# A sandwich layer in fp32 halves: one joined score product, k's high half written by ScalarE, and the joining of the weighted halves placed later

## The chip, the cores and the metric

One core of one Trainium2 chip runs the whole program. The metric is device time in microseconds of one execution; the number given is the median of the runs. TensorE (PE) multiplies and transposes, VectorE (DVE), ScalarE (ACT) and GpSimd (POOL) do the elementwise work, and SyncE (SP) issues the DMAs.

## The reference

x is 4 batches of 512 tokens, 1024 wide, 16 heads of 64. The program computes, all in fp32:

```
h = layernorm(x)
q, k, v = h @ Wq, h @ Wk, h @ Wv;  rotary embedding on q and k
attn = softmax(causal(q k^T) / 8);  a = (attn @ v) @ Wo
x = x + layernorm(a)
scores = 8 * softmax(layernorm(x) @ Wr^T + br)          # 8 experts
f = sum over experts of scores * ((h2 @ A^T) @ B), rank 16, times 2
out = x + layernorm(f)
```

## The kernel before, in words

An fp32 product is made of products of halves: each operand is split into a high half (a rounded copy) and a low half (the operand less the high half), and a product takes three terms: high with high, low with high, high with low. ScalarE makes the high half by a copy, VectorE or GpSimd the low one by a subtraction.

The attention part runs in 34 slots. A slot u belongs to one pair of heads (128 columns) and one batch; b = u mod 2 names the batch within the half of x that lies in SBUF. Slots 0 to 15 work on the first two batches, 16 to 31 on the other two. Each slot has 8 steps. In a step TensorE does 9 products of the projection of slot u (k, q and v of the pair of heads, 72 in all, three groups of 24), with the attention of the slot before woven in: the scores of one query tile of 128 rows (tile q = 0 to 7: head 0's four query tiles, then head 1's), the transposes of the probabilities of two tiles earlier, and twice a slot the product with v. A score tile i of a head has 128 * (i + 1) columns of keys, because of the causal mask. Step s of slot u works on score tile s - 1 of the slot before (`trailing(u, s, 1)`), so head 0's first tile comes in step 1 and head 1's in step 5.

Scores: `q_hl` holds q's high half in 64 partitions and its low half in the other 64. `k_hh` holds k's high half twice, in both halves of the partitions, so that one product gives (q high + q low) with k high. `k_lo` holds k's low half in its own partitions; the other 64 hold zeros, so that the second product adds q high with k low. Both go to the same columns of one bank and add up there.

The order of the work of each engine is written out by hand, step by step, in a function `slot` of each engine; every engine takes its instructions strictly in that order, and semaphores tie them. Per step and score tile the rank is:

- VectorE `negate` (line 1053): adds the mask to the scores, scales, writes them to `prob`, and gives the negated maximum of each row;
- ScalarE `exponent` (740): exponential with the row sum;
- VectorE `invert` (1063): reciprocal of the sum; GpSimd `divide` (595): the probabilities;
- TensorE `turn_probs` (1499) two steps later; ScalarE `pt_high` (751) and VectorE `pt_low` (1071) split the transposed tile.

Around it, in ScalarE's order: `v_raw` in step 0, `o_lower` (784) in steps 1 and 5, `v_high` in 2, `q_high` (761) in 3, `k_high` (766, both heads) in 6, and the high halves of the next weights (733) in steps 0, 4 and 6 (4 and 6 only with b = 1). In VectorE's: `rotate` (1080, the rotary embedding) in steps 3 and 6, `q_low` (1085) in 4 and 5, `k_low` (1091, 1092) of head 0 in 7 and of head 1 in step 0 of the next slot, `o_add` (1105) in 1 and 6. `o_lower` copies the lower product of the probabilities with v out of the bank, `o_add` adds it to the upper one. GpSimd makes the weights' sums (606, 607) and low halves (613), in steps 1 (b = 0), 2, 4, 5 and 7 (b = 1).

Slots 2 to 9 (`ahead`) also normalise and transpose the x of the other two batches: `x_variance`, `x_scale`, `ln_start`, `x_normal` and `hold_chunk` (in steps 4 and 7). In these slots `k_low` of head 0 stands before `invert` in step 7, in the others after `pt_low`.

Of the kernel before, what the change touches and what calls it, by code (L numbers as in the profile page):

```python
# [18 lines left out]
F32 = mybir.dt.float32  # L19
F32R = mybir.dt.float32r  # L20
# [4 lines left out]
P = 128  # L25
# [42 lines left out]
def sandwich_kernel(nc, x, wqkv, wo, ar, bt, br, cos, sin, scratch, out):  # L68
    with ExitStack() as ctx:
        def sb(stack, name, shape, dt=F32):  # L70
            return stack.enter_context(nc.sbuf_tensor(name, shape, dt))

        def sem(name):
            return ctx.enter_context(nc.semaphore(name))
# [61 lines left out]


        q_hl = sb(sB, "q_hl", [P, 2, 2, SEQ], F32R)
        k_hh = sb(sB, "k_hh", [P, 2, 2, SEQ], F32R)
        k_lo = sb(sB, "k_lo", [P, 2, 2, SEQ], F32R)  # L140
        w_sum = sb(sB, "w_sum", [P, EMBED])
        rope = sb(sB, "rope", [P, SEQ])
        rot = sb(sB, "rot", [P, SEQ])
# [9 lines left out]
        rinv = sb(sB, "rinv", [P, 4])  # L153
        o_low = sb(sB, "o_low", [DH, SEQ])
        o_sum = sb(sB, "o_sum", [DH, 2, SEQ])

        hold_hi = xin[:, 1, :].rearrange("p (c t) -> p c t", c=KC)
        hold_lo = xn[:, 1, :].rearrange("p (c t) -> p c t", c=KC)
# [63 lines left out]
        qk_lo_done = sem("qk_lo_done")  # L222
        s_done = sem("s_done")
        neg_done = sem("neg_done")
        exp_done = sem("exp_done")
        inv_done = sem("inv_done")
        prob_done = sem("prob_done")
# [66 lines left out]
        def real(u):  # L294

            return not isinstance(u, int) or 0 <= u < UNITS
# [399 lines left out]
        def _(act):  # L696
# [64 lines left out]
                    act.activation(q_hl[own, b, h, :], rot[own, :], ACT.Copy).then_inc(qk_hi_done, 1)  # L761

            def k_high(u, b, h):
                own = slice(DH * h, DH * h + DH)
                act.wait_ge(rot_done, 2 * u + 2)
                act.activation(k_hh[own, b, h, :], rot[own, :], ACT.Copy).then_inc(qk_hi_done, 1)

            def v_raw(u, b):
# [31 lines left out]
            def slot(pair, b, half, ahead=False):  # L800
# [6 lines left out]
                for s in range(STEPS):  # L807
                    exponent(u, s)
                    if s == 0 and real(u - 1):
                        v_raw(u - 1, 1 - b)  # L810
                    if s == 1 and real(u - 2):
                        o_lower(u - 2, 0)
                    if s == 5 and real(u - 2) and not (isinstance(u, int) and u > UNITS):
                        o_lower(u - 2, 1)
                    if s == 2 and real(u - 1):
                        v_high(u - 1, 1 - b, fill)
                    if prepares(u, ahead) and s == 6:
                        ln_start(ahead_tile(u) + 1)
                    pt_high(u, s)
                    if real(u):  # L820
                        if s == 0 and b == 0 and late(n, 1):
                            w_high(2, n)
                        if s == 3:
                            q_high(u, b)
                        if s == 6:
                            k_high(u, b, 0)
                            k_high(u, b, 1)
                        if b == 1 and not (isinstance(u, int) and u == UNITS - 1):
                            if s == 6:
                                w_high(1, n + 1)  # L830
# [157 lines left out]
        def _(dve):  # L988
# [56 lines left out]
            def negate(u, s):  # L1045
                a, q, g = trailing(u, s, 1)
                if real(a):
                    n = P * (q % QT + 1)
                    dve.wait_ge(s_done, g + 1)
                    if late(g, 4):  # L1050
                        dve.wait_ge(t_done, g - 3)
                    dve.sem_inc(gate_dve, 1)
                    dve.tensor_tensor_reduce(prob[:, q % 4, 0:n], sc_ps[q % 2][:, 0:n], mask[:, SEQ - n:SEQ],  # L1053
                                             -SOFT, 3e38, ALU.add, ALU.min, nmax[:, q % 4:q % 4 + 1]
                                             ).then_inc(neg_done, 1)

# [29 lines left out]
                                  ALU.subtract).then_inc(qk_lo_done, 1)  # L1086

            def k_low(u, b, h):
                own, other = slice(DH * h, DH * h + DH), slice(DH * (1 - h), DH * (1 - h) + DH)
                dve.wait_ge(qk_hi_done, 4 * u + 3 + h)  # L1090
                dve.tensor_tensor(k_lo[own, b, h, :], rot[own, :], k_hh[own, b, h, :].bitcast(F32), ALU.subtract)
                dve.tensor_copy(k_hh[other, b, h, :], k_hh[own, b, h, :]).then_inc(qk_lo_done, 1)  # L1092

            def v_low(u, b):
                dve.wait_ge(v_hi_done, u + 1)
# [28 lines left out]
            def slot(pair, b, half, ahead=False):  # L1124
# [4 lines left out]
                for s in range(STEPS):  # L1129
# [4 lines left out]
                        if s in (3, 6):  # L1134
                            rotate(u, b, s // 6)
                    closing = isinstance(u, int) and u >= UNITS
                    if s == 1 and real(u - 2) and not closing:
                        o_add(u - 2, 0)
                    if s == 6 and real(u - 2) and not (closing and u > UNITS):
                        o_add(u - 2, 1)  # L1140
                    leads = ahead or (isinstance(u, int) and u == UNITS - 1)
                    if leads and s == 7:
                        k_low(u, b, 0)
# [5 lines left out]
                    pt_low(u, s)  # L1149
                    if s == 0 and not closing and real(u - 1):  # L1150
                        k_low(u - 1, 1 - b, 1)
                    if closing and s == 1 and real(u - 2):
                        o_add(u - 2, 0)
                    if real(u):
                        if s in (4, 5):
                            q_low(u, b, s - 4)
                        if s == 7 and not leads:
                            k_low(u, b, 0)
# [240 lines left out]
        def _(pe):  # L1399
# [76 lines left out]
            def scores(u, s, b):  # L1476
                a, q, g = trailing(u, s, 1)
                if real(a):
# [5 lines left out]
                    if late(g, 2):  # L1484
                        pe.wait_ge(neg_done, g - 1)
                    qc, kc = slice(P * i, P * i + P), slice(0, P * i + P)
                    products(sc_ps[q % 2][:, kc], [(q_hl[:, ab, h, qc], k_hh[:, ab, h, kc]),
                                                   (q_hl[:, ab, h, qc], k_lo[:, ab, h, kc])], True, True
                             ).then_inc(s_done, 1)

            def turn_probs(u, s):
                a, q, g = trailing(u, s, 3)
# [270 lines left out]
```

## Time and profile before

| | us |
|---|---|
| median of 3 runs (1069.21 to 1069.33) | 1069.33 |
| the profiled execution's own time | 1069.58 |
| its span, first to last instruction | 1067.8 |
| TensorE busy | 1049.9 (98%) |
| VectorE busy | 756.9 (71%) |
| ScalarE busy | 591.3 (55%) |
| GpSimd busy | 439.4 (41%) |

The granted TensorE clock was 0.998 of full speed over the span. The attention slots run from about 41 us to 830 us. The ends of products are modelled in the profile, so the distance from start to start says what a product costs, and the busy share of TensorE is not its share of peak.

### The profile page before, as it was taken

The page shows a single profiled execution, that of the slowest core. Times are in us where ns is not written, and L with a number is a line of the kernel's source. Part 1 is how long each engine was busy: PE and PEld are TensorE (multiplying, and loading weights), DVE is VectorE, ACT ScalarE, POOL GpSimd, SP SyncE. Part 2 cuts the span into 40 slices and gives each one's busy share as a digit, 9 for nine tenths or more (in the row PEclk, how much of TensorE's full clock was granted, in tenths as well). Part 3 has the DMA queues.
Part 4 walks back from the last instruction along what each step waited for, and adds up shares of the span by engine and source line. Part 5 has one row for each costly group of instructions (what it writes and reads, how often), then busy time and mean ns, then how long its engine had stood idle before and what let it go on. Part 6 is the DMA issues. An engine that isn't in the chain of part 4 may idle for free.

```text
span 1067.8 us, 20069 instructions
## 1 busy us (share of the span) xinstructions
PE 1049.9 (98%) x5559; PEld 871.3 (82%) x5559; DVE 756.9 (71%) x2138; ACT 591.3 (55%) x1390; POOL 439.4 (41%) x422
## 2 busy tenths in 40 slices
PE   7999999999999999999999999999999999999996
PEld 6888888888888888888888888888877888888884
DVE  8777777776666666666666666666766877777777
ACT  7556666666555665565555655555576333333334
POOL 4153443435353635444452625344457232333221
PEclk9999999999999999999999999999999999999999
DMA  7022324241311256021111112020333323322311
GB/s 280 36 84 70 128 69 128 74 129 55 104 51 34 95 182 227 10 71 33 52 49 31 52 29 69 10 69 17 87 132 93 108 88 107 118 99 87 109 61 60
DMA packets 58663, 90.36 MB, mean 85 GB/s; under 512 B 3568, under 2 KB 36336, under 8 KB 58608
## 3 DMA queue, kind: packets, MB, share of 16 engines
q1 hardware_dynamic: 58464, 89.44, 25.9%
q8 instruction: 25, 0.41, 0.2%
q14 instruction: 30, 0.25, 0.1%
q10 hardware_dynamic: 144, 0.26, 0.1%
HBM read 64.52 MB, written 25.17 MB: 84 GB/s over the span
## 4 chain that ended last, share of the span: by engine, by line
PE 90%; DVE 3%; issue 2%; ACT 2%; POOL 0%; DVEq 0%; ACTq 0%; POOLq 0%
PE bank L1472 46%; PE bank L1403 25%; PE bank L1499 6%; PE bank L1518 3%; PE bank L1517 3%; PE bank L1633 2%; PE bank L1610 1%; PE bank L1445 1%; PE bank L1634 1%; PE bank L1520 1%; PE bank L1433 1%; ACT prob L740 1%; DVE prob L1053 0%; DVE k_hh L1092 0%; PE bank L1415 0%
## 5 line engine op out<-in xcount | busy, mean ns | idle before, releaser
L595 POOL TENSOR_SCALAR prob<-prob,rinv 128x128 f32<-128x128 f32 (+3 forms) x256 | 150.5, 588 | 436.8 <-DVE rinv L1063 436.8
L1472 PE MATMUL bank<-big_hi,w_hi 128*128 128x512 f32 (+1 forms) x776 | 329.4, 424 | 0.3 <-DVE big_lo L1034 0.3
L740 ACT ACTIVATE prob<-prob,nmax 128x128 f32<-128x128 f32 (+3 forms) x256 | 144.0, 562 | 304.3 <-DVE nmax L1053 302.7
L1472 PE MATMUL bank<-big_hi,w_lo 128*128 128x512 f32 (+1 forms) x776 | 304.5, 392 | 0.0
L1472 PE MATMUL bank<-big_lo,w_hi 128*128 128x512 f32 (+1 forms) x776 | 302.1, 389 | 0.0
L1472 PEld LDWEIGHTS bank<-big_hi,w_lo 128*128 128x128 f32 x776 | 145.6, 188 | 33.2
L1071 DVE TENSOR_TENSOR pT_lo<-bank,pT_hi 128x128 fp32r<-128x128 f32 (+3 forms) x256 | 123.7, 483 | 56.0 <-ACT pT_hi L751 53.3
L1472 PEld LDWEIGHTS bank<-big_hi,w_hi 128*128 128x128 f32 x776 | 146.6, 189 | 16.5 <-issue 0.4
L1472 PEld LDWEIGHTS bank<-big_lo,w_hi 128*128 128x128 f32 x776 | 147.1, 190 | 11.6
L1063 DVE RECIPROCAL rinv<-rsum 128x1 f32<-128x1 f32 x256 | 40.8, 159 | 129.3 <-ACT prob L740 128.9
L1053 DVE CUSTOM_DVE_ANT_0 prob<-bank,mask 128x128 f32<-128x128 f32 (+3 forms) x256 | 124.1, 485 | 9.2 <-PE bank L1403 5.1
L1499 PE MATMUL bank<-ident,prob 128*128 128x128 f32 x640 | 112.0, 273 | 1.5 <-POOL prob L595 1.0
L751 ACT ACTIVATE pT_hi<-bank 128x128 fp32r<-128x128 f32 (+3 forms) x256 | 108.8, 425 | 2.1 <-PE bank L1499 0.5
L1499 PEld LDWEIGHTS bank<-ident,prob 128*128 128x128 f32 x640 | 82.9, 141 | 32.5 <-POOL prob L595 6.0
L674 POOL TENSOR_TENSOR res<-res,x 128x1024 f32<-128x1024 f32 x14 | 33.4, 2389 | 146.1 <-ACT res L705 146.1
L613 POOL TENSOR_TENSOR w_lo<-w_sum,w_hi 128x1024 fp32r<-128x1024 f32 x32 | 83.0, 2593 | 8.0 <-ACT w_hi L733 7.7
L1403 PE MATMUL bank<-k_lo,q_hl 128*128 128x128 f32 (+3 forms) x256 | 82.2, 321 | 0.0
L1403 PE MATMUL bank<-k_hh,q_hl 128*128 128x128 f32 (+3 forms) x256 | 80.7, 315 | 0.5 <-DVE k_hh L1092 0.5
L1403 PE MATMUL bank<-big_hi,w_hi 128*128 128x512 f32 x192 | 79.5, 414 | 0.0
L1403 PE MATMUL bank<-big_lo,w_hi 128*128 128x512 f32 x192 | 75.2, 391 | 0.0
L1403 PE MATMUL bank<-big_hi,w_lo 128*128 128x512 f32 x192 | 75.0, 391 | 0.0
L1105 DVE TENSOR_TENSOR o_sum<-bank,o_low 64x512 f32<-64x512 f32 x64 | 43.3, 677 | 37.5 <-ACT o_low L784 37.5
(146 smaller groups left out, 1927.7 us busy)
## 6 DMA issues: line engine op xcount, KB each, us to landing
w_raw<-in_wqkv SPq DMA_DIRECT2D x48, 512.0 KB, 4.4
attention_out<-o_sum SPq DMA_DIRECT2D x64, 128.0 KB, 2.3
w_raw<-attention_out SPq DMA_DIRECT2D x16, 512.0 KB, 4.8
land<-in_x SPq DMA_DIRECT2D x16, 512.0 KB, 3.7
out<-res SPq DMA_DIRECT2D x14, 512.0 KB, 2.6
xin<-in_x SPq DMA_DIRECT2D x12, 512.0 KB, 5.7
xT_hold_hi<-xin SPq DMA_DIRECT2D x8, 512.0 KB, 3.6
xT_hold_lo<-xn SPq DMA_DIRECT2D x8, 512.0 KB, 5.4
```

The source lines that it names most:

```text
L595: pool.tensor_scalar(p, p, rinv[:, q % 4:q % 4 + 1], 1.0, ALU.mult, ALU.mult).then_inc(prob_done, 1)
L613: pool.tensor_tensor(w_lo[:, m, :], src, w_hi[:, m, :].bitcast(F32), ALU.subtract).then_inc(w_lo_done[m], 1)
L674: pool.tensor_tensor(res[:, i, :], res[:, i, :], x1[:, i, :], ALU.add).then_inc(res_done, 1)
L740: act.activation(prob[:, q % 4, 0:n], prob[:, q % 4, 0:n], ACT.Exp, scale=-1.0, bias=nmax[:, q % 4:q % 4 + 1], accum_out=rsum[:, q % 4:q % ...
L751: act.activation(pT_hi[:, h, 0:i + 1, P * i:P * i + P], pt_ps[q % 2][:, 0:P * (i + 1)].rearrange("p (j t) -> p j t", j=i + 1), ACT.Copy).t ...
L1053: dve.tensor_tensor_reduce(prob[:, q % 4, 0:n], sc_ps[q % 2][:, 0:n], mask[:, SEQ - n:SEQ], -SOFT, 3e38, ALU.add, ALU.min, nmax[:, q % 4:q ...
L1063: dve.reciprocal(rinv[:, q % 4:q % 4 + 1], rsum[:, q % 4:q % 4 + 1]).then_inc(inv_done, 1)
L1071: dve.tensor_tensor(pT_lo[at], pt_ps[q % 2][:, 0:P * (i + 1)].rearrange("p (j t) -> p j t", j=i + 1), pT_hi[at].bitcast(F32), ALU.subtract ...
L1105: dve.tensor_tensor(o_sum[:, h, :], o_ps[0:DH, :], o_low[:, :], ALU.add).then_inc(osum_done, 1)
L1403: mm = pe.matmul(dst, lhsT, rhs, start=first and n == 0, stop=last and n == len(terms) - 1)
L1472: done = pe.matmul(grp_ps[(b + k) % 2][:, cols], w, xt[:, cols], start=at == 0, stop=at == GROUP_MM - 1)
L1499: last = pe.transpose(pt_ps[q % 2][:, P * j:P * j + P], prob[:, q % 4, P * j:P * j + P], ident[:, :])
```

## The change

`k_hh` and `k_lo` become the two parts of one tile `k_all`. For the first query tile of each head (128 columns of keys) one product of 256 columns replaces the two of 128: it writes q with k high into columns 0 to 127 and q with k low into columns 128 to 255 of bank `sc_ps[0]`. VectorE adds the second 128 columns to the mask into a new tile `low_masked`, waits for that, and passes it to `negate` in place of the mask. The copy of k's high half into the other half of the partitions moves from VectorE (a `tensor_copy` in `k_low`) to ScalarE (an activation in `k_high`). `o_lower` and `o_add` move behind `pt_high` and `pt_low` of the same step.

```diff
-        k_hh = sb(sB, "k_hh", [P, 2, 2, SEQ], F32R)
-        k_lo = sb(sB, "k_lo", [P, 2, 2, SEQ], F32R)
+        k_all = sb(sB, "k_all", [P, 2, 2, 2, SEQ], F32R)
+        k_hh, k_lo = k_all[:, 0, :, :, :], k_all[:, 1, :, :, :]
...
             def k_high(u, b, h):
                 act.wait_ge(rot_done, 2 * u + 2)
+                act.activation(k_hh[other, b, h, :], rot[own, :], ACT.Copy)
                 act.activation(k_hh[own, b, h, :], rot[own, :], ACT.Copy).then_inc(qk_hi_done, 1)
...
                     exponent(u, s)
-                    if s == 1 and real(u - 2):
-                        o_lower(u - 2, 0)
-                    if s == 5 and real(u - 2) and not (isinstance(u, int) and u > UNITS):
-                        o_lower(u - 2, 1)
...
                     pt_high(u, s)
+                    if s == 1 and real(u - 2):
+                        o_lower(u - 2, 0)
+                    if s == 5 and real(u - 2) and not (isinstance(u, int) and u > UNITS):
+                        o_lower(u - 2, 1)
...
                     dve.sem_inc(gate_dve, 1)
-                    dve.tensor_tensor_reduce(prob[:, q % 4, 0:n], sc_ps[q % 2][:, 0:n], mask[:, SEQ - n:SEQ],
+                    added = mask[:, SEQ - n:SEQ]
+                    if q % QT == 0:
+                        added = low_masked[:, :]
+                        dve.tensor_tensor(added, sc_ps[0][:, P:2 * P], mask[:, SEQ - P:SEQ], ALU.add).then_inc(low_added, 1)
+                        dve.wait_ge(low_added, 2 * a + q // QT + 1)
+                        dve.sem_inc(gate_dve, 1)
+                    dve.tensor_tensor_reduce(prob[:, q % 4, 0:n], sc_ps[q % 2][:, 0:n], added,
...
             def k_low(u, b, h):
-                dve.tensor_tensor(k_lo[own, b, h, :], rot[own, :], k_hh[own, b, h, :].bitcast(F32), ALU.subtract)
-                dve.tensor_copy(k_hh[other, b, h, :], k_hh[own, b, h, :]).then_inc(qk_lo_done, 1)
+                dve.tensor_tensor(k_lo[own, b, h, :], rot[own, :], k_hh[own, b, h, :].bitcast(F32), ALU.subtract
+                                  ).then_inc(qk_lo_done, 1)
...
-                    if s == 1 and real(u - 2) and not closing:
-                        o_add(u - 2, 0)
-                    if s == 6 and real(u - 2) and not (closing and u > UNITS):
-                        o_add(u - 2, 1)
...
                     pt_low(u, s)
...
-                    if closing and s == 1 and real(u - 2):
+                    if s == 1 and real(u - 2):
                         o_add(u - 2, 0)
+                    if s == 6 and real(u - 2) and not (closing and u > UNITS):
+                        o_add(u - 2, 1)
...
-                    products(sc_ps[q % 2][:, kc], [(q_hl[:, ab, h, qc], k_hh[:, ab, h, kc]),
-                                                   (q_hl[:, ab, h, qc], k_lo[:, ab, h, kc])], True, True
-                             ).then_inc(s_done, 1)
+                    if i == 0:
+                        pe.matmul(sc_ps[0][:, 0:2 * P].rearrange("p (a n) -> p a n", a=2), q_hl[:, ab, h, qc],
+                                  k_all[:, :, ab, h, kc], start=True, stop=True).then_inc(s_done, 1)
+                    else:
+                        products(sc_ps[q % 2][:, kc], [(q_hl[:, ab, h, qc], k_hh[:, ab, h, kc]),
+                                                       (q_hl[:, ab, h, qc], k_lo[:, ab, h, kc])], True, True
+                                 ).then_inc(s_done, 1)
```

## Rows read from the trace of the kernel before

**Rows 1.** Page, part 1: engine, busy us (share), instructions.
```profile
PE 1049.9 (98%) x5559; PEld 871.3 (82%) x5559; DVE 756.9 (71%) x2138; ACT 591.3 (55%) x1390; POOL 439.4 (41%) x422
```
**Rows 2.** Waits: who waited for whom, us in total, times, longest.
```profile
DVE prob L1053 <- PE bank L1403: 5.1, 4, 2.3
...
DVE mv L996 <- DVE stats L1182: 3.2, 21, 0.2
```
**Rows 3.** Timeline, TensorE, later slots: start us, duration us, instruction.
```profile
508.65 0.22 PE L1403 MATMUL bank<-k_hh,q_hl 128*128 128x128 f32 x1
...
750.25 0.22 PE L1403 MATMUL bank<-k_hh,q_hl 128*128 128x128 f32 x1
```
**Rows 4.** Timeline, VectorE, masking of the tiles of rows 3.
```profile
512.03 0.29 DVE L1053 CUSTOM_DVE_ANT_0 prob<-bank,mask 128x128 f32<-128x128 f32 x1
...
753.27 0.29 DVE L1053 CUSTOM_DVE_ANT_0 prob<-bank,mask 128x128 f32<-128x128 f32 x1
```
**Rows 5.** Timeline, TensorE, early slots, first score tiles of three slots.
```profile
114.04 0.22 PE L1403 MATMUL bank<-k_hh,q_hl 128*128 128x128 f32 x1
...
139.70 0.22 PE L1403 MATMUL bank<-k_hh,q_hl 128*128 128x128 f32 x1
...
164.73 0.22 PE L1403 MATMUL bank<-k_hh,q_hl 128*128 128x128 f32 x1
```
**Rows 6.** Timeline, TensorE, 399.8 to 403 us, a first and a second score tile.
```profile
399.83 0.22 PE L1403 MATMUL bank<-k_hh,q_hl 128*128 128x128 f32 x1
...
400.28 0.40 PE L1472 MATMUL bank<-big_lo,w_hi 128*128 128x512 f32 x1
...
402.58 0.28 PE L1403 MATMUL bank<-k_lo,q_hl 128*128 128x256 f32 x1
...
402.94 0.39 PE L1472 MATMUL bank<-big_lo,w_hi 128*128 128x512 f32 x1
```
**Rows 7.** Groups by line and shape: busy us, mean ns of one, idle before.
```profile
L784 ACT ACTIVATE o_low<-bank 64x512 f32<-64x512 f32 x64 | 38.1, 596 | 2.3 <-PE bank L1520 0.8
...
L1092 DVE CAST k_hh<-k_hh 64x512 fp32r<-64x512 f32 x64 | 35.4, 552 | 0.9
```
**Rows 8.** Timeline, ScalarE, step 6 of later slots, b = 1 and b = 0.
```profile
503.28 1.28 ACT L766 ACTIVATE k_hh<-rot 64x512 fp32r<-64x512 f32 x2
...
505.55 0.60 ACT L740 ACTIVATE prob<-prob,nmax 128x384 f32<-128x384 f32 x1
...
527.41 1.27 ACT L766 ACTIVATE k_hh<-rot 64x512 fp32r<-64x512 f32 x2
528.75 0.62 ACT L740 ACTIVATE prob<-prob,nmax 128x384 f32<-128x384 f32 x1
```
**Rows 9.** Timeline, VectorE, step 7 of the later slot with b = 1.
```profile
507.33 0.72 DVE L1092 CAST k_hh<-k_hh 64x512 fp32r<-64x512 f32 x1
```
**Rows 10.** Timeline, ScalarE, step 6 of early slots, b = 0 and b = 1.
```profile
186.10 1.27 ACT L766 ACTIVATE k_hh<-rot 64x512 fp32r<-64x512 f32 x2
188.15 0.62 ACT L740 ACTIVATE prob<-prob,nmax 128x384 f32<-128x384 f32 x1 [0.78 <-DVE nmax L1053]
...
211.41 1.27 ACT L766 ACTIVATE k_hh<-rot 64x512 fp32r<-64x512 f32 x2
...
213.68 0.60 ACT L740 ACTIVATE prob<-prob,nmax 128x384 f32<-128x384 f32 x1
```
**Rows 11.** Timeline, GpSimd and VectorE, step 5 of a later slot with b = 1.
```profile
499.86 0.38 POOL L595 TENSOR_SCALAR prob<-prob,rinv 128x128 f32<-128x128 f32 x1
500.20 1.05 POOL L606 TENSOR_TENSOR w_sum<-w_raw 128x512 f32<-128x512 f32 x1
...
500.22 1.57 DVE L1085 TENSOR_TENSOR q_hl<-rot,q_hl 64x512 fp32r<-64x512 f32 x1
```
**Rows 12.** Timeline, GpSimd and VectorE, 311 to 315 us.
```profile
311.58 2.87 POOL L613 TENSOR_TENSOR w_lo<-w_sum,w_hi 128x1024 fp32r<-128x1024 f32 x1
...
312.17 2.57 DVE L1092 CAST k_hh<-k_hh 64x512 fp32r<-64x512 f32 x1
```

More of the change, by code:

```diff
@@ L155, in sandwich_kernel @@
         o_sum = sb(sB, "o_sum", [DH, 2, SEQ])
+        low_masked = sb(sB, "low_masked", [P, P])
         hold_hi = xin[:, 1, :].rearrange("p (c t) -> p c t", c=KC)
@@ L224, in sandwich_kernel @@
         neg_done = sem("neg_done")
+        low_added = sem("low_added")
         exp_done = sem("exp_done")
@@ L763, in k_high @@
             def k_high(u, b, h):
-                own = slice(DH * h, DH * h + DH)
+                own, other = slice(DH * h, DH * h + DH), slice(DH * (1 - h), DH * (1 - h) + DH)
                 act.wait_ge(rot_done, 2 * u + 2)
+                act.activation(k_hh[other, b, h, :], rot[own, :], ACT.Copy)
                 act.activation(k_hh[own, b, h, :], rot[own, :], ACT.Copy).then_inc(qk_hi_done, 1)
@@ L1088, in k_low @@
             def k_low(u, b, h):
-                own, other = slice(DH * h, DH * h + DH), slice(DH * (1 - h), DH * (1 - h) + DH)
+                own = slice(DH * h, DH * h + DH)
                 dve.wait_ge(qk_hi_done, 4 * u + 3 + h)
-                dve.tensor_tensor(k_lo[own, b, h, :], rot[own, :], k_hh[own, b, h, :].bitcast(F32), ALU.subtract)
-                dve.tensor_copy(k_hh[other, b, h, :], k_hh[own, b, h, :]).then_inc(qk_lo_done, 1)
+                dve.tensor_tensor(k_lo[own, b, h, :], rot[own, :], k_hh[own, b, h, :].bitcast(F32), ALU.subtract
+                                  ).then_inc(qk_lo_done, 1)
             def v_low(u, b):
```

## The prediction, made before the changed kernel was seen

> **What bounds the kernel now.** I read the totals of the page first. TensorE is busy for 98% of the span [rows 1], so any nanosecond taken from it looks like a nanosecond of the kernel. The second view, the waits, makes me doubt that: VectorE waited for TensorE's scores only 4 times, 5.1 us in all [rows 2], although it has 256 score tiles to read. An engine fed by TensorE that never waits for it is either far too slow, or running behind at a pace of its own.
>
> So I read the timeline twice, five pairs of slots apart. TensorE starts the first score tile of a head at 508.65 us and the one ten slots on at 750.25: 24.16 us a slot, 48.32 a pair [rows 3]. VectorE's masking of the same two tiles starts at 512.03 and 753.27: 48.25 a pair [rows 4]. It begins 3.4 us after its scores at the first and 3.0 us at the second, and creeps up by 0.07 us a pair. A follower that was paced by TensorE would keep its distance; this one runs free. The loop is VectorE's masking, ScalarE's exponential, VectorE's reciprocal and low half, the next masking; both engines take their work in a written order and the time goes into waiting for each other. It has 0.07 us a pair in hand over TensorE, no more. In the early slots (2 to 9, which also prepare the second half's x) it is already the slower one: of two slots one takes TensorE 25.03 us (139.70 to 164.73) and the other 25.66, 0.63 of it waiting, so that a pair takes 50.69 and not 50.06 [rows 5]. The kernel has two bounds of nearly one height, and a change to either counts only if it doesn't raise the other. I therefore price the change in both.
>
> **On TensorE: the joined product.** Before, from the start of the first of two 128-column products to the second 512-column product behind them took 400.28-399.83 = 0.45 us; from one 256-column product over the same 512 it is 402.94-402.58 = 0.36 [rows 6]. A joined product saves 0.09 to 0.10 us, taken as 0.098, and there are 64 (32 slots, two heads): 6.3 us. Bounds: 0, if two separate blocks of columns stream worse than one, and 0.22, the whole pair. The Trainium skill ("TensorE: Matmul & The Clock Gate", section "Wait — 56ns, not 53.3ns?") speaks against even this: by its spacing for warm products, two of 128 columns take 111 ns and one of 256 about 109, so joining would give nothing. The rows show otherwise, since the product after the short pair starts late.
>
> **On the loop, first heads' tiles.** A masked block needs an addition of the same shape and operands as the masking, which takes 0.29 us [rows 4], and then a wait of VectorE for itself. The nearest such wait is that of the variance behind its statistics, 3.2 us over 21 cases, 0.15 each [rows 2]. Together 0.44 us, twice a slot (bounds 0.2 and 0.6). Behind that wait stand the masking, the reciprocal and the low half, and ScalarE's exponential waits for them.
>
> **The dropped copy and the two new ones.** VectorE's copy of k's high half goes: 0.55 us in the mean, 0.72 in step 7 beside a division of GpSimd [rows 7, 9], so about 0.4 in step 0. There it stood directly before the masking, so it pays for the new addition: 0. In step 7 ScalarE now writes four halves in place of two, which adds 1.27 us (a pair takes 1.27 or 1.28 [rows 8]) ahead of the exponential of the same step.
> - Later slots with b=1: the exponential follows the copies and the weight's high half without a gap (503.28, 505.55 [rows 8]), so it is 1.27 late. Reciprocal, low half and k's low half follow it; the copy saves 0.72 there [rows 9]. Net +0.53.
> - Later slots with b=0: the exponential followed at 528.75 on copies that ended at 528.68 [rows 8], so 1.23 late, less 0.72: +0.51.
> - Early slots with b=1: k's low half is made while VectorE waits anyway, so the copy was free and its going gives nothing; the high half of the held x and its low half stand behind the exponential (211.41, 213.68 [rows 10]): +1.27.
> - Early slots with b=0: the exponential waited for its masking until 188.15, 0.78 after the copies' end [rows 10]. The copies now end at 188.64; the masking, behind the moved addition of the halves, at 188.70. Net +0.59.
>
> **The moved joining.** In step 1 ScalarE's rank of work is the same and VectorE must still do the addition before the next masking: 0, though the reciprocal comes 1.2 us sooner and relieves the tightest turn of TensorE. In step 5 ScalarE's 0.60 us [rows 7] leaves the path of pT's halves: -0.60+0.44 = -0.16, say -0.18 with its gap. In step 6 the moved addition is hidden by the four copies.
>
> **The lock between VectorE and GpSimd.** In step 5 of later b=1 slots q's low half starts at 500.22 and takes 1.57 us, because GpSimd's sum of weights, begun at 500.20, held it until 501.25; after that it needed 0.54 [rows 11]. Coming 0.18 us sooner, it would stand first in the rank, behind the short division alone, which ends at 500.24, and be done at 500.8 to 500.9: -0.94 for the step in place of -0.18. The 2.57 us copy at 312.17, which sat out GpSimd's 2.87 us [rows 12], goes altogether: -2.15 once. On the other side GpSimd's longest piece moves 1.27 us later in b=1 slots and then meets k's low half of head 1: +0.16. The Trainium skill ("SBUF — State Buffer", section "SBUF: two separate sides") states that a VectorE instruction with two SBUF inputs and a GpSimd one exclude each other for the whole instruction, whoever starts first. By that rule, the trace agrees: who is first is decided here by 0.02 us.
>
> **The sum.** Early pair: b=0 gives 0.59-0.18 = 0.41, b=1 gives 1.27 (its step 5 stays blocked by GpSimd): 1.68 us on a loop that is already the bound. Four pairs: 6.7. Later pair: b=0 gives 0.51-0.18 = 0.33, b=1 gives 0.53-0.94+0.16 = -0.25: +0.08, ten pairs: 0.8. Once: -2.15. Together +5.3, less 0.3 where TensorE alone is the bound (the first slots). TensorE's 6.3 us are not seen: they become waiting. The profiled execution took 1069.58 us (span 1067.8 and 1.8 around it), 0.25 above the median of the runs. 1069.58+5.0 = 1074.6 us.
>
> **The rivals.**
> - *TensorE is the pace after all (the other side).* Then ScalarE's two extra copies fill idle time, and the moved joining feeds TensorE's tightest turns sooner. For it: 98% busy, ScalarE 55%. Against: the creep of 0.07 us a pair. It decides as soon as the loop comes below 49.7 us in an early pair and 47.9 in a later one. 1069.58-6.3 = 1063.3, less part of the four times 0.6 us that early pairs lose now: 1062.5. Chance 0.20.
> - *The lock is not won.* q's low half still comes behind the sum of weights; each later pair costs 0.94 more: 1074.6+9.4 = 1084.0. For it: a tie of hundredths, and the loop shifts against GpSimd every pair. Against: VectorE asks while the division still runs. 0.15.
> - *Half hidden.* The early slots pay, but the later ones keep the loop below TensorE's new 47.9 us: 6.7-2.15 less 4 of TensorE's saving: 1066 to 1071, centre 1069. For it: VectorE stands 3 us behind its scores and could lose some of that before TensorE feels it. Against: that is spent once, not per pair. 0.15.
> - *The change doesn't do what it says:* two blocks at an 8 KB distance stream no faster. TensorE then saves nothing, and since it is not the bound the time is that of the forecast; it takes the first rival's gain away.
>
> **How the numbers follow.** Forecast 0.50, own range 1071 to 1078. About 0.2% (2.1 us) is what can be told from no change. Faster: the first rival's 0.20 and a third of the third, 0.25. Same: another third, 0.05. Slower: 0.70. The range runs from 1063 to 1083; outside it lie a good half of the first rival and of the second, 0.18.
>
> **What would show it.** Starts of the early first score tiles 52.4 us a pair apart instead of 50.7, and later ones at 48.4; four copies of k's high half taking 2.5 us, the exponential behind them; TensorE waits of 1 to 2 us an early pair, put down to the division or k's low half; the 256-column product followed after 0.12 us; q's low half of step 5 at 0.8 us in place of 1.57. I am wrong if early pairs take less than 50.7: then the loop had room that I didn't see; and if later pairs take 49.4, the lock went the other way.

## The result, and the profile after

The kernel before was run again beside the changed one.

| | before | changed |
|---|---|---|
| median, us | 1069.27 (1069.13 to 1069.33) | 1083.17 (1082.88 to 1083.45) |
| profiled execution, span, us | 1069.58, 1067.8 | 1083.45, 1081.7 |

The ratio is 1.013, interval 1.0113 to 1.0148: slower by 13.9 us, where 5.0 were forecast. The direction was right, and the time lies 0.17 us outside the range of 1063 to 1083.

Page of the changed kernel, busy time by engine, and the chain that ended last, by engine:

```profile
PE 1050.6 (97%) x5495; PEld 862.0 (80%) x5495; DVE 745.2 (69%) x2138; ACT 634.8 (59%) x1454; POOL 443.7 (41%) x422
...
PE 62%; ACT 13%; issue 11%; DVE 10%; DVEq 1%; ACTq 0%; POOL 0%; POOLq 0%
```

Against [rows 1] VectorE does 11.7 us less work, ScalarE 43.5 us more, and TensorE has 64 products fewer and is busy as long as before (the ends are modelled). The chain now runs over ScalarE and VectorE for nearly a quarter of its length. The waits (who waited for whom, us in total, times, longest):

```profile
DVE prob L1062 <- DVE low_masked L1059: 13.1, 64, 0.6
...
PEld bank L1510 <- POOL prob L597: 8.7, 17, 1.6
...
PE bank L1510 <- DVE pT_lo L1080: 4.1, 10, 1.2
...
PE bank L1495 <- DVE k_all L1100: 3.6, 10, 0.9
...
DVE low_masked L1059 <- PE bank L1495: 3.0, 1, 3.0
DVE prob L1062 <- PE bank L1410: 2.1, 2, 1.3
```

The last two rows say that VectorE still hardly waits for scores: 5.1 us in 3 cases, after 5.1 in 4 before [rows 2]. And TensorE now waits for what the loop of VectorE and ScalarE makes: the probabilities, their low half, k's low half. The timeline of TensorE, first score tiles of the slots of [rows 5] and [rows 3]:

```profile
116.04 0.28 PE L1495 MATMUL bank<-k_all,q_hl 128*128 128x256 f32 x1
116.15 0.39 PE L1479 MATMUL bank<-big_hi,w_hi 128*128 128x512 f32 x1
116.38 0.40 PE L1479 MATMUL bank<-big_lo,w_hi 128*128 128x512 f32 x1
...
169.04 0.28 PE L1495 MATMUL bank<-k_all,q_hl 128*128 128x256 f32 x1
...
518.98 0.38 PE L1495 MATMUL bank<-k_all,q_hl 128*128 128x256 f32 x1 [0.23 <-DVE k_all L1100]
...
761.27 0.38 PE L1495 MATMUL bank<-k_all,q_hl 128*128 128x256 f32 x1 [0.15 <-DVE k_all L1100]
```

The early pair from 116.04 to 169.04 takes 53.00 us (before 50.69, forecast 52.4); the later ones 48.46 (before 48.32, forecast 48.4), and TensorE starts the joined product only when VectorE has k's low half: it is the follower now. The joined product with the 512-column one behind it takes 116.38-116.04 = 0.34 us, before 0.45 [rows 6]. Over all 64 places the median of this distance falls from 0.45 to 0.35. So the saving of TensorE is there, and the total doesn't show it.

VectorE's timeline, step 5 of a later slot with b=1 and, last, the masking that answers to the second of [rows 4]:

```profile
508.63 0.29 DVE L1059 TENSOR_TENSOR low_masked<-bank,mask 128x128 f32<-128x128 f32 x1
509.12 0.29 DVE L1062 CUSTOM_DVE_ANT_0 prob<-bank,low_masked 128x128 f32<-128x128 f32 x1 [0.19 <-DVE low_masked L1059]
...
510.94 0.82 DVE L1094 TENSOR_TENSOR q_hl<-rot,q_hl 64x512 fp32r<-64x512 f32 x1
...
765.13 0.29 DVE L1062 CUSTOM_DVE_ANT_0 prob<-bank,low_masked 128x128 f32<-128x128 f32 x1 [0.19 <-DVE low_masked L1059]
```

From the addition's start to the masking's are 0.49 us, 0.20 of them idle. And GpSimd's for the same step, where its sum of weights now comes second and is stretched itself:

```profile
510.86 0.36 POOL L597 TENSOR_SCALAR prob<-prob,rinv 128x128 f32<-128x128 f32 x1
511.20 1.47 POOL L608 TENSOR_TENSOR w_sum<-w_raw 128x512 f32<-128x512 f32 x1
```

The tie of [rows 11] (500.20 against 500.22) is won: q's low half stands in front and takes 0.82 in place of 1.57.

In an early slot with b=1 it is lost, as forecast. The same step there (VectorE and GpSimd), and ahead of it ScalarE's step 6 of an early slot with b=0:

```profile
192.04 0.63 ACT L768 ACTIVATE k_all<-rot 64x512 fp32r<-64x512 f32 x1
192.69 0.63 ACT L769 ACTIVATE k_all<-rot 64x512 fp32r<-64x512 f32 x1
193.34 0.63 ACT L768 ACTIVATE k_all<-rot 64x512 fp32r<-64x512 f32 x1
193.98 0.63 ACT L769 ACTIVATE k_all<-rot 64x512 fp32r<-64x512 f32 x1
194.64 0.62 ACT L742 ACTIVATE prob<-prob,nmax 128x384 f32<-128x384 f32 x1
...
214.54 1.04 POOL L608 TENSOR_TENSOR w_sum<-w_raw 128x512 f32<-128x512 f32 x1
...
214.79 1.33 DVE L1094 TENSOR_TENSOR q_hl<-rot,q_hl 64x512 fp32r<-64x512 f32 x1
```

The four copies take 2.57 us and the exponential follows without a gap, where it had waited 0.78 for its masking [rows 10].

**Where the 13.9 us are.** I cut both traces at the starts of the masking of head 0's first tile (`prob` from the 128-column bank). a is the slot whose scores they are, masked in slot a+1:

| stretch | before | changed | more | forecast |
|---|---|---|---|---|
| start to a=1 | 67.6 | 69.0 | +1.4 | -0.3 |
| a=1 to 9, four early pairs | 201.5 | 210.8 | +9.4 | +6.7 |
| a=9 to 11, with the 2.57 us copy | 49.7 | 48.6 | -1.0 | -2.1 |
| a=11 to 29, nine later pairs | 434.6 | 436.6 | +2.1 | +0.7 |
| a=29 to the end | 314.5 | 316.5 | +2.0 | 0 |

The same cut finer: medians over the slots of a kind (a = 3 to 6 for the early ones, 11 to 28 for the later ones), us from the masking of tile q to the next.

```
                 0>1   1>2   2>3   3>4   4>5   5>6   6>7   7>0   sum
early b=0 before 2.71  2.77  1.77  4.61  3.30  3.32  2.60  3.94  25.03
          after  2.56  2.91  1.79  5.09  2.54  4.05  2.68  3.99  25.60
early b=1 before 2.71  2.77  1.77  4.62  3.59  3.32  2.86  3.95  25.60
          after  2.56  2.91  1.79  5.09  3.19  4.05  3.70  3.99  27.28
later b=0 before 2.71  2.77  1.77  3.37  3.31  2.21  3.13  3.95  23.22
          after  2.56  2.91  1.79  3.83  2.54  2.93  3.09  3.98  23.64
later b=1 before 2.71  2.77  1.77  3.37  4.20  2.21  4.04  3.95  25.03
          after  2.56  2.91  1.79  3.83  2.69  2.93  4.10  4.02  24.83
```

An early pair costs 2.25 more (forecast 1.68), a later one 0.22 (forecast 0.08). 3>4 holds the new addition and wait: +0.46 to +0.48, forecast 0.44. 7>0 holds the second one and, against it, the dropped copy: +0.03 to +0.07, forecast 0. 4>5 holds the moved `o_lower`, and 5>6 the moved `o_add`: +0.73, which the prediction had put under the four copies (e7 tests that). All numbers below that name a pair come from such a table of their own kernel.

### The profile page after: what moved, and what is told of

It reads as the page before. It is cut to its first block, busy times and chain, and to the rows that moved or that the text cites. A ratio compares the mean times of both kernels' runs of the same rounds, so it can differ in the third digit from the quotient of the medians.

```text
span 1081.7 us, 20091 instructions
## 1 busy us (share of the span) xinstructions
PE 1050.6 (97%) x5495; PEld 862.0 (80%) x5495; DVE 745.2 (69%) x2138; ACT 634.8 (59%) x1454; POOL 443.7 (41%) x422
## 4 chain that ended last, share of the span: by engine, by line
PE 62%; ACT 13%; issue 11%; DVE 10%; DVEq 1%; ACTq 0%; POOL 0%; POOLq 0%
PE bank L1479 28%; PE bank L1410 20%; PE bank L1510 4%; ACT prob L742 3%; ACT pT_hi L753 2%; DVE q_hl L1094 2%; DVE prob L1062 2%; PE bank L1644 2%; ACT k_all L769 2%; ACT k_all L768 2%; PE bank L1529 2%; PE bank L1528 1%; PE bank L1621 1%; DVE k_all L1100 1%; PE bank L1452 1%
## 5 line engine op out<-in xcount | busy, mean ns | idle before, releaser
L597 POOL TENSOR_SCALAR prob<-prob,rinv 128x128 f32<-128x128 f32 (+3 forms) x256 | 155.1, 606 | 446.3 <-DVE rinv L1072 445.5
L1479 PE MATMUL bank<-big_hi,w_hi 128*128 128x512 f32 (+1 forms) x776 | 326.1, 420 | 0.3 <-DVE big_lo L1037 0.3
L1062 DVE CUSTOM_DVE_ANT_0 prob<-bank,mask 128x256 f32<-128x256 f32 (+2 forms) x192 | 105.4, 549 | 4.0 <-PE bank L1410 2.1
L1410 PE MATMUL bank<-k_all,q_hl 128*128 128x256 f32 (+2 forms) x384 | 100.1, 342 | 0.0
L615 POOL TENSOR_TENSOR w_lo<-w_sum,w_hi 128x1024 fp32r<-128x1024 f32 x32 | 80.7, 2521 | 9.2 <-ACT w_hi L735 8.9
L1410 PEld LDWEIGHTS bank<-k_all,q_hl 128*128 128x128 f32 x384 | 69.7, 188 | 13.3
L1529 PE MATMUL bank<-pT_lo,v_hl 128*64 128x512 f32 (+3 forms) x256 | 62.1, 309 | 0.0
```

Source lines behind the costliest of these rows:

```text
L597: pool.tensor_scalar(p, p, rinv[:, q % 4:q % 4 + 1], 1.0, ALU.mult, ALU.mult).then_inc(prob_done, 1)
L615: pool.tensor_tensor(w_lo[:, m, :], src, w_hi[:, m, :].bitcast(F32), ALU.subtract).then_inc(w_lo_done[m], 1)
L1410: mm = pe.matmul(dst, lhsT, rhs, start=first and n == 0, stop=last and n == len(terms) - 1)
L1479: done = pe.matmul(grp_ps[(b + k) % 2][:, cols], w, xt[:, cols], start=at == 0, stop=at == GROUP_MM - 1)
L1529: pe.matmul(o_ps[0:DH, cols], v_hl[:, b, j, h, 0:DH], pT_lo[:, h, j, cols], start=False, stop=False)
```

## The experiments

"Before" in brackets is the kernel before on the same chip in the same batch, and ratios are to it, with their intervals. An expectation calls the forecast's account theory L (the loop sets the pace) and its rivals by other letters. The first four experiments take the change apart.

**e1: the join alone.** Only the tile `k_all`, the joined product, the addition and its wait, on the kernel before.

```diff
+                        dve.tensor_tensor(added, sc_ps[0][:, P:2 * P], mask[:, SEQ - P:SEQ], ALU.add).then_inc(low_added, 1)
+                        dve.wait_ge(low_added, 2 * a + q // QT + 1)
...
+                        pe.matmul(sc_ps[0][:, 0:2 * P].rearrange("p (a n) -> p a n", a=2), q_hl[:, ab, h, qc],
+                                  k_all[:, :, ab, h, kc], start=True, stop=True).then_inc(s_done, 1)
```


> Only the joined product with VectorE's masked addition; VectorE still copies k's high half, the joining of the weighted halves stays where it was. Theory L (the loop of VectorE and ScalarE sets the pace): the addition and the wait put 0.48 us into the loop twice a slot, 0.96 a slot, with nothing taken out, over some 30 slots 25 us or more: 1069 + 20 to 30 = 1090 to 1099 us. Theory T (TensorE sets the pace, and the changed kernel is slow for its copies alone): 64 times 0.1 us saved, 1063 us.

Measured 1095.58 us [1070.16], ratio 1.0237 (1.022 to 1.0254). An early pair takes 53.19, a later one 49.67. 25.4 us for an edit that takes 6.3 us off TensorE: most of the price of 64 places (0.48 each would be 31). GpSimd's lock now falls better in later b=1 slots (4>5 takes 3.70 in place of 4.20) and worse in early ones (4.19 in place of 3.59).

**e2: ScalarE's copies alone.**

```diff
+                act.activation(k_hh[other, b, h, :], rot[own, :], ACT.Copy)
...
-                dve.tensor_copy(k_hh[other, b, h, :], k_hh[own, b, h, :]).then_inc(qk_lo_done, 1)
```


> Only the copies: ScalarE writes k's high half into both halves of the partitions, VectorE's copy goes. Theory L: early pairs of slots cost 1.27 and 0.5 us for the later exponential and gain 0.44 twice in step 0, +0.9 a pair; later pairs +0.53 and +0.51 less 0.88, +0.2, of which 0.07 is free: 1071 to 1075 us. Theory S (the two extra copies are the whole slowdown): 1083.

Measured 1075.88 [1070.16], 1.0056 (1.0039 to 1.0073). Early pair 51.84, later 48.54. 6>7 grows by 0.68 (b=0) and 1.43 (b=1) in early slots, where 0.59 and 1.27 were forecast, and 7>0 shrinks by 0.44. 44 us more work for ScalarE, which was 55% busy, cost 5.7 us, and 38 us less for VectorE don't pay for it. The time is a little above the 1071 to 1075 expected.

**e3: the moves alone.** `o_lower` behind `pt_high`, `o_add` behind `pt_low`.

```diff
-                    if s == 6 and real(u - 2) and not (closing and u > UNITS):
-                        o_add(u - 2, 1)
...
                     pt_low(u, s)
...
+                    if s == 6 and real(u - 2) and not (closing and u > UNITS):
+                        o_add(u - 2, 1)
```


> Only the order: o_lower and o_add behind pt_high and pt_low. Theory L: step 5 gets 0.6 us shorter, step 6 0.6 to 0.7 longer where nothing hides the moved addition, the step-5 lock is won in later slots with b=1; the loop stays as fast as TensorE in the later slots, early pairs within 0.5 of 50.7: 1067 to 1070 us. Theory M (the moved addition of step 6 is the whole slowdown): 1083.

Measured 1065.47 [1070.16], 0.9957 (0.994 to 0.9974), below the 1067 to 1070 expected. Early pair 50.12, later 48.32. One row of its waits answers to the first of [rows 2]:

```profile
DVE prob L1053 <- PE bank L1401: 20.8, 40, 2.3
```

40 times in place of 4: with the moves VectorE has caught up with TensorE in the later slots, which pace at 48.32. This is what a kernel looks like in which VectorE follows TensorE. TensorE's own pace is no other than before: 48.32 a later pair in both [rows 3]. Before, the two were level there, with VectorE 3 us behind; the moves gain in the early pairs, whose stretch shrinks by 2.9 us, and once by the lag that is made up (1.7 in the later stretch).

**e4: all but the join.** The changed kernel with two products of 128 columns, and without the addition.

```diff
-                    if i == 0:
-                        pe.matmul(sc_ps[0][:, 0:2 * P].rearrange("p (a n) -> p a n", a=2), q_hl[:, ab, h, qc],
-                                  k_all[:, :, ab, h, kc], start=True, stop=True).then_inc(s_done, 1)
```


> The changed kernel with the two products of 128 columns and the plain mask put back. Theory L: 0.96 us a slot leaves the loop; later pairs come below TensorE's 48.3 us and are paced by it, early pairs fall from 52.9 to 51.0: 1069 to 1072 us, faster than the changed kernel although TensorE works 6.3 us more. Theory T: 1083 + 6.3 = 1089 us.

Measured 1067.78 [1070.16], 0.9977 (0.9968 to 0.9987), again below the expectation. The rest of the change is slightly faster than before. The join on top of it costs 1083.17-1067.78 = 15.4 us (by the two ratios to before, 16), the whole loss and more. A rival in which TensorE's saving counts, at 1089 for this kernel, falls.

**e5: the join without its addition.** The joined product on the kernel before; the low block is never added, so this leaves out k's low half in the first tile of each head.


> Only the joined product, and VectorE masks its first 128 columns with the plain mask: the product with k's low half is computed but left out of the scores of each head's first tile (its addition and the wait go). So TensorE saves and the loop carries nothing new. Theory L: the loop keeps its 50.6 and 48.25 us a pair, 0.07 us a pair and the few stalls of TensorE's own are to be had: 1067 to 1070 us. Theory T: 64 times 0.1 us are seen, 1063.5 us. Theory P (the joined product itself streams slower and is part of the 25 us of the join alone): above 1072.

```diff
 against e1:
-                        added = low_masked[:, :]
-                        dve.tensor_tensor(added, sc_ps[0][:, P:2 * P], mask[:, SEQ - P:SEQ], ALU.add).then_inc(low_added, 1)
-                        dve.wait_ge(low_added, 2 * a + q // QT + 1)
```

Measured 1069.16 [1069.67], 0.9996 (0.9986 to 1.0005): 6.3 us less TensorE are worth nothing on the kernel before. The forecast's "not seen" is shown here. That "they become waiting" is shown in part: TensorE's busy time falls by 2.9 us (1047.0 for 1049.9) in a span 0.8 shorter.

**e8: the same with the moves.** Also without the low block.


> The kernel with the moved order alone, with the joined product and again without the addition of its second part (left out of the scores). There the loop is shorter than TensorE's work in the later slots. Theory L: now TensorE's saving is seen, 0.39 us a pair in some 10 to 14 pairs, and less in the early ones: 1059.5 to 1062 us, against 1065.5 for the order alone. If the joined product saved nothing on TensorE: 1065.5.

```diff
 against e3:
+                    if i == 0:
+                        pe.matmul(sc_ps[0][:, 0:2 * P].rearrange("p (a n) -> p a n", a=2), q_hl[:, ab, h, qc],
+                                  k_all[:, :, ab, h, kc], start=True, stop=True).then_inc(s_done, 1)
+                    else:
...
```

Measured 1060.6 [1069.67], 0.9918 (0.9901 to 0.9934); later pair 47.9. Against e3 the join's product now gives 4.9 us (their ratios to before, 0.9918 and 0.9957, put it at 4.2), and the pair comes to the 47.9 that the prediction gave for TensorE alone. The saving is real; it needs a loop with room. By the spacing between like products in the Trainium skill ("TensorE: Matmul & The Clock Gate", section "Wait — 56ns, not 53.3ns?"), as an estimate, nothing would come of it. TensorE's timeline of the kernel before, at its very first score tile, and then that of the changed kernel:

```profile
41.81 0.22 PE L1403 MATMUL bank<-k_hh,q_hl 128*128 128x128 f32 x1
41.87 0.27 PE L1403 MATMUL bank<-k_lo,q_hl 128*128 128x128 f32 x1
41.98 0.45 PE L1472 MATMUL bank<-big_hi,w_hi 128*128 128x512 f32 x1
42.26 0.39 PE L1472 MATMUL bank<-big_lo,w_hi 128*128 128x512 f32 x1
```
```profile
42.39 0.28 PE L1495 MATMUL bank<-k_all,q_hl 128*128 128x256 f32 x1
42.51 0.40 PE L1479 MATMUL bank<-big_hi,w_hi 128*128 128x512 f32 x1
42.75 0.39 PE L1479 MATMUL bank<-big_lo,w_hi 128*128 128x512 f32 x1
```

The rule's spacing shows between the two short products (0.06 us), but 0.11 pass to the next and 0.28 to the one behind that, where the joined one has 0.12 and 0.24: 0.45 against 0.36.

**e12: the addition, unread.** The join alone, but the masking takes the mask and doesn't wait; the low block is added into a tile that nobody reads.

```diff
 against e1:
-                        added = low_masked[:, :]
...
-                        dve.wait_ge(low_added, 2 * a + q // QT + 1)
-                        dve.sem_inc(gate_dve, 1)
```


> The kernel with the join alone, where VectorE still makes the masked addition but masks with the plain mask and so doesn't wait for it (the low part of each head's first tile is added up and left out). It parts the 0.48 us of that step into the addition and the wait. Theory L with 0.29 for the addition and 0.19 for the wait: 0.38 us a slot leaves a kernel that is bound by the loop everywhere, 28 to 32 slots: 1095.6 - 10.6 to 12.2 = 1083.4 to 1085. If the addition overlaps the masking behind it by 0.08 us, as neighbours on VectorE without a wait do: 1079 to 1081. If the wait costs nothing: 1095.

Measured 1076.76 [1069.53], 1.0065 (1.0049 to 1.008), below all three times of the expectation. VectorE's timeline:

```profile
501.35 0.29 DVE L1057 TENSOR_TENSOR low_masked<-bank,mask 128x128 f32<-128x128 f32 x1
501.56 0.28 DVE L1058 CUSTOM_DVE_ANT_0 prob<-bank,mask 128x128 f32<-128x128 f32 x1
```

3>4 and 7>0 grow by 0.20 each against 0.48 with the wait. The addition of 0.29 us costs 0.20, since the masking starts 0.08 before its end when nothing ties them; the wait (with the counter increment that goes with it) costs 0.28, and with it 1095.58-1076.76 = 18.8 us of the join's 25. The prediction (0.15) and the expectation (0.19) both took the wait for cheaper than it is. The Trainium skill ("VectorE: DVE Perf Modes", section "The DRAIN you can't avoid") says of eight copies in a row that a semaphore after each costs nothing extra; here, where VectorE waits for the one in front, 64 of them cost 0.28 us each, and the measurement decides.

**e6: head 1's copies in step 7** of the changed kernel.

```diff
                             k_high(u, b, 0)
-                            k_high(u, b, 1)
+                        if s == 7:
+                            k_high(u, b, 1)
```


> The changed kernel with head 1's two copies of k's high half in step 7, behind pT's high half, in place of step 6. Theory L: in later slots the exponential of step 7 comes 1.27 us sooner and ScalarE has its idle time behind it; the loop falls below TensorE's 47.9 us a pair: -0.5 us a pair, 10 pairs. In early slots the copies now stand before the held x's high half, on which VectorE waits: nothing. 1076 to 1080 us. Rival (ScalarE's total work counts, not its place): 1083 unchanged.

Measured 1079.95 [1069.67], 1.0096 (1.008 to 1.0113). Later pairs drop to TensorE's 47.9, which the expectation had; early ones rise from 52.88 to 54.7, which it had not: 6>7 grows from 2.68 to 4.03 (b=0) and from 3.70 to 4.11 (b=1). The waits say why. Step 7 of these slots also carries a chunk of the held x, whose high half ScalarE now makes behind the two copies, and VectorE waits for it before its next masking. The same row of the changed kernel, then of e6:

```profile
DVE xn L1045 <- ACT xin L725: 1.6, 8, 0.2
```
```profile
DVE xn L1046 <- ACT xin L725: 13.0, 8, 1.6
```

The expectation had named this place and priced it at nothing. That the time still lies within 1076 to 1080 is luck: the early pairs cost 6.8 us and the rest of the attention slots gains more than was expected.

**e7: step 6's `o_add` back in front of the reciprocal,** on the changed kernel.

```diff
+                    if s == 6 and real(u - 2) and not (closing and u > UNITS):
+                        o_add(u - 2, 1)
                     leads = ahead or (isinstance(u, int) and u == UNITS - 1)
```


> The changed kernel with o_add of step 6 put back in front of the reciprocal. Theory L: 0.7 us leaves the stretch from tile 5 to tile 6 and comes back in the next, since the exponential of step 7 waits for the four copies, not for the masking: 1082 to 1083.5. Theory M (the moved addition costs where it stands): 0.7 us a slot over 28 slots, 1064 to 1070.

Measured 1083.18 [1069.67], 1.0126 (1.0109 to 1.0143): the same. 5>6 gets 0.6 shorter and 6>7 0.6 longer. Beside four copies it doesn't matter whether the addition stands before the reciprocal or behind `pt_low`, as forecast: the two stretches together are as long as with the move.

**e9 and e10: the moves but step 6's, and the join on that.** e7 suggests that step 6's move costs where there are only two copies.

```diff
 e9, against e3:
                     closing = isinstance(u, int) and u >= UNITS
+                    if s == 6 and real(u - 2) and not (closing and u > UNITS):
+                        o_add(u - 2, 1)
...
                         o_add(u - 2, 0)
-                    if s == 6 and real(u - 2) and not (closing and u > UNITS):
-                        o_add(u - 2, 1)
```


> The moved order, but o_add of step 6 stays in front of the reciprocal; all else as in the kernel before. Theory L: the loop is 0.7 us a slot shorter than with all moves, but there TensorE already set the pace (50.1 and 48.3 us a pair): about the same, 1064 to 1065.5. If the moves' gain came from step 6: back to 1069.

Measured 1065.03 [1069.53], 0.9957 (0.9943 to 0.997), the ratio of e3, as expected: where TensorE sets the pace, step 6's move costs nothing.

e10 adds to e9 the joined product, its addition and its wait in every slot.


> The same order with the joined product and its addition in every slot; VectorE keeps the copy. Theory L: in later slots the loop has room, 23.4 + 24.5 = 47.9 us, the pace is TensorE's new 47.9: -3.9 us over 10 pairs; early pairs 48.9 + 1.9 = 50.8 against 50.06: +3.5 us. Together 1063 to 1066.5. If the join cost 25 us wherever it stands: 1090.

Measured 1074.08 [1069.53], 1.0041 (1.0026 to 1.0057): far off. The join costs 9 us even without ScalarE's copies, and I had expected none. 8.4 of it stand in the four early pairs (51.70 a pair, 50.8 expected), 2.4 in start and tail, and the pair from a=9 to 11 gives 2.4 back. A part of the early excess is in the b=1 slot, where 4>5 takes 3.19 and not 2.55 as in b=0 (VectorE and GpSimd):

```profile
211.52 1.05 POOL L608 TENSOR_TENSOR w_sum<-w_raw 128x512 f32<-128x512 f32 x1
...
211.78 1.33 DVE L1093 TENSOR_TENSOR q_hl<-rot,q_hl 64x512 fp32r<-64x512 f32 x1
```

**e11: join where there is room.** e9, with the joined product, addition and wait in slots 10 to 29 alone. It computes everything.

```diff
+        def joined(u, ahead):
+            return not ahead and not (isinstance(u, int) and (u < 2 * AHEAD + 2 or u >= UNITS - 2))
...
-                    if i == 0:
+                    if joined(u, ahead) and i == 0:
```


> As the one before, but joined in slots 10 to 29 alone, where the loop has room; slots 0 to 9 and 30 to 33 keep two products. The whole computation. Theory L: early slots as without the join, later ones at TensorE's 47.9 us a pair: 1065 - 3.9 = 1060.5 to 1062. If the room in the later slots is not there: 1065 or more.

Measured 1062.8 (1062.41 to 1063.0) [1069.53], 0.9936 (0.9922 to 0.995): the fastest complete kernel of the study, 2.2 us below e9, with later pairs of 48.11. It beats both kernels. The expectation was 1060.5 to 1062, with later pairs at 47.9.

**e13: the changed kernel, joined in slots 10 to 29 alone,** with the same function `joined`.


> The changed kernel with the joined product, its addition and its wait only in slots 10 to 29; the first slots, the early slots and the last two go back to two products of 128 columns. My account puts the join's 15.4 us (1083.18 for the change against 1067.78 without the join) so: start 0.9, four early pairs 2.5 each, the last slots some 1.4, the rest in the later slots. By that account this kernel shows early pairs of 50.3 to 50.4 us, later pairs of 48.4 to 48.5, and 1070 to 1072. Rival: the loss is handed on from slot to slot whichever slots make it (the later pairs then grow when the early ones shrink): 1076 or more.

Measured 1069.75 [1070.09], 0.9998 (0.9988 to 1.0008), a little below the account. Early pairs 50.33, later ones 48.42. Against the changed kernel the span is 14.2 us shorter: 0.8 up to a=1, 10.3 in the four early pairs, 2.2 behind a=29, and 0.9 between. Nothing is handed on: the rival falls. The tail's loss is the join's; of the start's 1.4 us the join has 0.8, and e4, the change without it, has 0.5 more than before there.

**e14: the second sum of weights in step 6,** on the changed kernel.

```diff
-                        if s in (2, 5):
-                            w_pairs(s // 5, n + 1)
+                        if s in (2, 6):
+                            w_pairs(s // 6, n + 1)
```


> The changed kernel, but GpSimd makes its second sum of weights in step 6 in place of step 5. If q's low half is blocked in the early slots with b = 1 by this sum, and the step is on the loop there, that low half takes 0.8 us in place of 1.33 and an early pair gets shorter by 0.5 to 0.6: 1080.5 to 1081.5 in all, later pairs as before. Rival: the loop in the early slots waits for something else, or the sum now holds the four copies' reader in step 6 (k's low half in step 7) just as long: 1083 +- 0.5.

Measured 1080.22 [1070.09], 1.0095 (1.0078 to 1.0112), just below the 1080.5 to 1081.5 expected. VectorE and GpSimd in step 5 of the early b=1 slot:

```profile
212.98 0.37 POOL L597 TENSOR_SCALAR prob<-prob,rinv 128x128 f32<-128x128 f32 x1
...
213.58 0.69 DVE L1094 TENSOR_TENSOR q_hl<-rot,q_hl 64x512 fp32r<-64x512 f32 x1
...
216.21 1.04 POOL L608 TENSOR_TENSOR w_sum<-w_raw 128x512 f32<-128x512 f32 x1
```

0.69 in place of 1.33, 4>5 at 2.55 in place of 3.19, the early pair at 52.30 and 2.6 us less over the four pairs. The low half is on the loop and the lock lengthens it. By the Trainium skill ("SBUF — State Buffer", section "SBUF: two separate sides"), whoever starts first holds the other off: the trace agrees, in 1.33 behind the sum and in GpSimd's 1.47 when it comes second.

## Why the prediction was right in kind and wrong in size

**The bound: right.** e5 (6.3 us off TensorE are worth 0.5, by the interval 1.5 at most), e3 (40 waits for scores as soon as the loop has room) and e8 (the saving appears) show the two bounds: the loop above TensorE in early slots, the two level in later ones. The rival "TensorE is the pace after all" is out.

**The edits one by one: mostly right.** Addition and wait 0.48 for 0.44, but split otherwise (0.20 and 0.28 for 0.29 and 0.15). The copies 0.68 and 1.43 for 0.59 and 1.27. `o_lower` off the path: -0.76 in 4>5 of b=0 slots for -0.60, and -0.40 in early b=1 slots, where the lock keeps the rest (with the addition, step 5 comes out at +0.07 there, forecast 0). `o_add`'s +0.73 in 5>6 comes back in 6>7, as forecast (e7): together the two stretches grow by 0.81 for 0.59 in b=0 early slots and by 1.57 for 1.27 in b=1, of which e2 has 0.68 and 1.43 by the copies alone. The lock of the later b=1 slots was won by 0.26 us: 4>5 falls by 1.51, of it 0.75 by q's low half itself. That such a tie of 0.02 us fell as forecast is no proof of more than that the shift was larger than the tie. The rival against it was priced too high: without the lock a later pair loses 0.94-0.18 = 0.76 and not 0.94, and 1074.6+7.6 = 1082.2 is inside the range, where 1084.0 was not.

**The step that failed is the sum:** start and tail were put at nothing, the copies in early slots were taken too short, and the lock was counted as won once too often. It had 5.0 and should have had 13.9; the 8.9 between are the differences of the last two columns of the first table:
- *Start, 1.7, and tail, 2.0.* The sum had -0.3 at the start, "where TensorE alone is the bound", and nothing for the tail, without a reason. e1 alone has +1.3 at the start and +2.2 in the tail, e13 without the join there has +0.7 and -0.1. The five additions that fall behind the cut at a=29 cost 0.45 each: the loop bounds in the tail as well. At the start the join has about half of the loss, the rest of the change the other. I had checked the pace in the early and the later slots and taken it for granted outside.
- *Early pairs, 2.7.* Mis-sized by 0.57 a pair in slots 3 to 6 (and by 0.9 in the last of the four pairs): of the 0.57, 0.52 in 5>6 and 6>7. There the copies cost 2.11 a pair by themselves (e2) where 1.86 was in the sum; the other 0.27 comes with the whole change and stays open, and it is not the moved addition (e7).
- *Later pairs, 1.4,* 0.22 for 0.08 a pair: the terms that nearly cancel there are 0.42 for 0.33 and -0.20 for -0.25.
- *The pair of the long copy, 1.1.* Its going did give what was forecast: 6>7 of that slot (a=10) falls from 6.30 to 4.12. But the sum also counted the lock as won once in each of the ten later pairs, and in this slot q's low half had not been held before, since GpSimd's sum of weights started only at 306.40. VectorE's timeline of the kernel before:

```profile
305.49 0.71 DVE L1085 TENSOR_TENSOR q_hl<-rot,q_hl 64x512 fp32r<-64x512 f32 x1
```

So 4>5 falls by 0.41 in this slot (from 3.33 to 2.92), and not by the 1.51 of the other later b=1 slots: that is the 1.1.

All these stretches err to one side. The single terms don't: `o_lower` and the lock gave more than was forecast. What weighs is costs taken at their bare duration, or at nothing where I had not looked, and a gain counted once too often.

Not settled: the 0.13 to 0.14 us in each early slot that neither e2 nor e7 explains, and the 0.6 us by which TensorE comes later to its very first score tile (42.39 for 41.81).

## What to carry to other kernels

When an engine is 98% busy and its consumer never waits for it, look for a second loop, and compare paces and not shares: an edit that trades 0.1 us of the busy engine for 0.48 us in that loop loses wherever both are level. Make such a trade only in the stages in which the trace shows room (here slots 10 to 29, and after the moves: 1062.8), and read start and tail for the same loop before counting them at nothing. A wait of an engine for its own last instruction has to be priced like an instruction: here 0.28 us beside an addition of 0.29.

## What the runs showed of the hardware

- VectorE's wait for its own addition of 128 columns costs as much as the addition (0.29 us): 0.20 us idle in the trace, 0.28 from start to start, since without a wait the next instruction begins 0.08 before the end of the one ahead (e12).
- VectorE's subtraction for q's low half, when it meets GpSimd's sum of weights, takes 1.33 or 1.57 us for 0.69; the sum itself takes 1.47 for 1.04 when it comes second. Shifts of 0.3 us decide which.
- Two 128-column products in place of one of 256 cost TensorE 0.10 us although they start 0.06 apart: the products behind them come late.
